# A Gram matrix's mirrored part: identity matmuls on TensorE against 32x32 transposes on VectorE and a round trip through DRAM

## What is computed

```python
# layer 0: softmax attention; q, k have 64 rows, v has 512
q = (Wq @ x + bq).T;  k = Wk @ x2 + bk;  v = Wv @ x2 + bv
attn = softmax(q @ k)          # (1024, 1024), over the keys
x = v @ attn.T + x
# layer 1: attention without softmax
g = (g_w @ x2 + g_b).T; theta = (theta_w @ x + theta_b).T; phi = phi_w @ x2 + phi_b
y = ((theta @ phi) / phi.shape[-1] @ g).T
wy = w_w @ y + w_b
out = bn_gamma * (wy - bn_mean) * rsqrt(bn_var + eps) + bn_beta + x
```

## Time and profile before

| | |
|---|---|
| median of 3 runs | 1039.71 us (1039.63 to 1039.83) |
| profiled execution | 1039.65 us, span 1037.8 us |
| PE busy | 1028.6 us, 99% |
| DVE, ACT, POOL busy | 685.1, 494.9, 296.4 us (66, 48, 29%) |
| moved by DMA | 155.46 MB |

### The profile page before, as it was taken

The page is one execution under the profiler, slowest core; times in us unless marked ns, Lnnn a source line. Parts: engine busy times, 40 slices in busy tenths (PEclk is TensorE's granted clock), DMA queues, the critical chain, the costliest instruction groups (busy, mean ns, idle before and its releaser), DMA issues.

```text
span 1037.8 us, 13692 instructions
## 1 busy us (share of the span) xinstructions
PE 1028.6 (99%) x5055; PEld 850.6 (82%) x5055; DVE 685.1 (66%) x970; ACT 494.9 (48%) x835; POOL 296.4 (29%) x253
## 2 busy tenths in 40 slices
PE   9999999999999999999999999999999999999998
PEld 7778888888888887888888888888887888878887
DVE  6994497834888258882588825887268862688625
ACT  7653564425554264542744427454275532655321
POOL 1652370122701236012360123502144022540220
PEclk9999999999999999999999999999999999999999
DMA  7747153561545514455244552455434464335602
GB/s 255 217 142 234 65 200 123 163 222 54 170 129 189 190 63 161 139 186 183 72 153 152 178 178 87 137 163 181 165 103 136 150 201 142 122 123 163 193 31 81
DMA packets 94226, 155.46 MB, mean 150 GB/s; under 512 B 10064, under 2 KB 43728, under 8 KB 94160
## 3 DMA queue, kind: packets, MB, share of 16 engines
q1 hardware_dynamic: 84944, 137.80, 40.6%
q10 hardware_dynamic: 9216, 16.78, 4.8%
HBM read 104.22 MB, written 50.33 MB: 149 GB/s over the span
## 4 chain that ended last, share of the span: by engine, by line
PE 89%; DVE 4%; POOL 2%; DMA 2%; ACT 1%; issue 1%; SPq 0%; ACTq 0%; DVEq 0%
PE pG L661 33%; PE pG L567 14%; PE pG L672 8%; PE pG L575 6%; PE pG L606 4%; PE pG L582 4%; PE pT L694 3%; PE pG L694 3%; PE pS L618 2%; PE pM L649 2%; PE pT L514 2%; PE pT L618 2%; PE pM L640 2%; PE pS L503 2%; POOL x1s L1067 1%; DMA x2T_f<-in_ctx2T_dram 1%
## 5 line engine op out<-in xcount | busy, mean ns | idle before, releaser
L661 PE MATMUL pG<-pt,vT 128*128 128x512 f32 x1536 | 353.8, 389 | 0.0
L661 PEld LDWEIGHTS pG<-pt,vT 128*128 128x128 f32 x1536 | 286.9, 188 | 58.6
L1103 POOL TENSOR_TENSOR xms<-xr,xms 128x512 fp32r<-128x512 f32 x64 | 87.4, 1372 | 327.6 <-ACT xms L854 327.6
L567 PE MATMUL pG<-wv,x2s 128*128 128x512 f32 x720 | 169.3, 392 | 0.3
L567 PEld LDWEIGHTS pG<-wv,x2s 128*128 128x128 f32 x720 | 133.9, 188 | 31.7 <-issue 2.5
L1019 DVE SCALAR_TENSOR_TENSOR xr<-pG,cl,xr 128x512 f32<-128x512 f32 x64 | 47.9, 749 | 167.8 <-PE pG L661 167.8
L854 ACT ACTIVATE xms<-xr 128x512 fp32r<-128x512 f32 x64 | 40.4, 631 | 174.9 <-DVE xr L1019 174.9
L996 DVE TENSOR_TENSOR pt<-mv,pt 128x512 fp32r<-128x512 f32 x128 | 83.3, 693 | 56.3 <-ACT pt L832 56.1
L1099 POOL TENSOR_TENSOR ys<-yf,ys 128x256 fp32r<-128x256 f32 x32 | 29.6, 926 | 284.0 <-ACT ys L823 284.0
L832 ACT ACTIVATE pt<-mv 128x512 fp32r<-128x512 f32 x128 | 73.3, 622 | 57.9 <-DMA mv<-turn 42.0
L1074 POOL TENSOR_TENSOR x2Ts<-x2T_f,x2Ts 128x512 fp32r<-128x512 f32 x64 | 86.2, 1374 | 37.3 <-ACT x2Ts L792 37.3
(11 more groups left out here) (145 smaller groups left out, 1486.6 us busy)
## 6 DMA issues: line engine op xcount, KB each, us to landing
turn<-tp SPq DMA_DIRECT2D x64, 512.0 KB, 3.2
mv<-turn SPq DMA_DIRECT2D x256, 128.0 KB, 2.9
x2T_f<-in_ctx2T_dram SPq DMA_DIRECT2D x32, 512.0 KB, 4.8
xr<-in_x_dram ACTq DMA_DIRECT2D x64, 256.0 KB, 5.2
st<-in_ctx_dram SPq DMA_DIRECT2D x31, 512.0 KB, 6.4
st<-in_x_dram SPq DMA_DIRECT2D x29, 512.0 KB, 4.2
out_dram<-oh SPq DMA_DIRECT2D x32, 256.0 KB, 2.0
out_dram<-xr SPq DMA_DIRECT2D x31, 256.0 KB, 8.0
```

The lines of the kernel that those rows point to most:

```text
L567: last = mm(bank, x2s[:, l, c, 128 * m:128 * m + 128], wv[:, r, c, :], start=(c == 0 and n == 0), stop=(c == 3 and n == 2))
L661: last = mm(bank, vT[:, l, m, 128 * c:128 * c + 128], pt(h)[:, r, m, :], start=(m == 0 and n == 0), stop=(m == 7 and n == 2))
L1103: done(tt(xms(h)[:, c, LO, :], xr[c][:, :], xms(h)[:, c, HI, :].bitcast(F), ALU.subtract), "xlo")
```

## The change

In images 1 to 7 the eleven identity matmuls go. ACT's do_L writes L into gram_n; DVE transposes each row block of it in 32x32 blocks (do_tl) into tl; SP writes tl to a DRAM scratch `nt` and reads it back with four DMAs into lt; DVE adds lt to gram_f in SBUF (do_gn), after its do_G. The PE transposes GT, ACT's do_G and what follows wait for do_gn (s_gn). The division by the row sums moves from DVE to ACT (do_n; DVE keeps the reciprocal, do_r). The four strings of order are written anew; of the waits of do_tr, that on s_mv becomes one on s_turn. The first image keeps its identity matmuls, with two small swaps in its order.

```diff
-   PE  "... v:0 v:1 psi v:2 S:0 S:1 L:0 L:1 L:2 S:2 S:3 L:3 G:0 G:1 G:2 GT:0 G:3 GT:1 S:4 S:5 v:3 v:4 v:5 v:6 v:7
-        Y:0 S:6 S:7 Y:1 Y:2 Y:3 PV:0,0,0 M:0 ..."
+   PE  "... v:0 v:1 v:2 S:0 S:1 L:0 psi L:1 L:2 S:2 S:3 L:3 G:0 G:1 G:2 G:3 S:4 S:5 v:3 v:4 v:5 GT:0 GT:1 v:6 v:7
+        Y:0 S:6 S:7 Y:1 Y:2 Y:3 PV:0,0,0 M:0 ..."
-   ACT "... acc x2T:5 q v:0 x2T:6 x2T:7 q2 v:1 k2 v:2 S:0 L:0 L:1 S:1 L:2 L:3 S:2 G:0 S:3 G:1 T:0 GT:0 G:2 G:3 GT:1
-        v:3 T:1 v:4 S:4 v:5 v:6 T:2 v:7 S:5 Y:0 T:3 Y:1 Y:2 Y:3 psi S:6 S:7 xr:0 ..."
+   ACT "... x2T:5 q v:0 x2T:6 x2T:7 q2 v:1 k2 acc v:2 S:0 L:0 n:0 L:1 S:1 L:2 n:1 S:2 L:3 n:2 S:3 n:3 T:0 G:0 G:1
+        G:2 G:3 v:3 S:4 n:4 v:4 T:1 S:5 v:5 GT:0 GT:1 n:5 v:6 T:2 v:7 T:3 Y:0 S:6 Y:1 n:6 Y:2 Y:3 psi S:7 n:7 xr:0 ..."
-   DVE "acc k q accl v:0 q2 v:1 k2 S:0 v:2 S:1 n:0 tr:0 n:1 tr:1 S:2 S:3 G:0 n:2 G:1 tr:2 G2:0 G:2 G:3 n:3 G2:1 T:0
-        tr:3 G2:2 G2:3 v:3 GT:0 S:4 v:4 GT:1 T:1 v:5 n:4 S:5 v:6 tr:4 T:2 v:7 Y:0 n:5 tr:5 Y:1 T:3 Y:2 Y:3 S:6 S:7
-        n:6 tr:6 n:7 tr:7 mt ..."
+   DVE "acc k q v:0 q2 v:1 k2 accl S:0 v:2 S:1 r:0 tr:0 tl:0 r:1 tl:1 tr:1 tl:2 S:2 S:3 r:2 tl:3 G:0 tr:2 G:1 r:3 G:2
+        G:3 tr:3 T:0 S:4 gn:0 gn:1 gn:2 gn:3 r:4 v:3 G2:0 G2:1 tr:4 S:5 G2:2 G2:3 v:4 r:5 T:1 v:5 GT:0 GT:1 tr:5 v:6
+        T:2 v:7 T:3 S:6 Y:0 r:6 Y:1 tr:6 S:7 Y:2 Y:3 r:7 tr:7 mt ..."
@@ SP, move(b, p)
+                if b and p == 0:
+                    eng.wait_ge(s_tl, 4 * b)
+                    eng.dma_start(nt, tl[:, :, :]).then_inc(s_nw, 16)
                 for t in range(2):
                     eng.wait_ge(s_turn[2 * p + t], 16 * (b + 1))
                 for k in range(2):
+                    if b and p == 0 and k == 1:
+                        eng.wait_ge(s_nw, 16 * b)
+                        for i in range(4):
+                            eng.dma_start(lt[32 * i:32 * i + 32, :, :], nt[:, i, :].rearrange("(j a) n -> a j n", a=32))\
+                                .then_inc(s_nr, 16)
@@ PE, do_G and do_GT
-                       x2Ts[:, HI, m, G_FROM[r]:512], start=(m == 0), stop=False)
+                              x2Ts[:, HI, m, G_FROM[r]:512], start=(m == 0), stop=(b > 0 and m == 7))
+                if b:
+                    done(last, "g")
+                    return
-                wait_free(eng, b, use_g(b, r))
+                if b:
+                    eng.wait_ge(s_gn, 4 * (b - 1) + r + 1)
@@ ACT: do_v, do_L, do_n, do_G
+                elif m >= 3 and b:
+                    eng.wait_ge(s_nw, 16 * b)
+                done(act(gram_n[:, r, :] if b else gram[:, LO, r, :], bank_of(use_l(b, r)), ACT.Copy), "Lhi")
+            def do_n(b, t):
+                wait(eng, "rec", b, t)
+                done(act(P[:, :], P[:, :], ACT.Copy, scale=rec[:, t:t + 1]), "norm")
             def do_G(b, r):
+                if b:
+                    eng.wait_ge(s_gn, 4 * (b - 1) + r + 1)
@@ DVE: do_tl, do_gn, and do_tr for t >= 4
+            def do_tl(b, r):
+                wait(eng, "Lhi", b, r)
+                n = 256 if r < 2 else 512
+                eng.transpose(tl_row(r), gram_n[:, r, 0:n].rearrange("p (c i m) -> p i c m", i=4, m=32))\
+                    .then_inc(s_tl, 1)
+            def do_gn(b, r):
+                eng.wait_ge(s_nr, 64 * b)
+                if r == 0:
+                    wait_free(eng, b, use_g(b, 3))
+                for i in range(2):
+                    d = max(G_FROM[r] // 128 - 2 * i, 0)
+                    if d < 2:
+                        part = gram_f[r][:, 256 * i:256 * i + 256].rearrange("p (d j m) -> p d j m", d=2, j=4)[:, d:]
+                        last = tt(part, part, lt_pair(i, r)[:, d:], ALU.add)
+                last.then_inc(s_gn, 1)
-                    for i in range(2):
-                        eng.wait_ge(s_mv[t // 2 * 2 - 4 + i], 64 * (b + 1))
+                    eng.wait_ge(s_turn[t - 4], 16 * (b + 1))
```

More of the change, by code:

```diff
@@ L199, in xattn_kernel @@
         mts = at("mts", [128, 2, 2, 256], R, rd + 12288)
+        gram_n = at("gram_n", [128, 4, 512], F, rd + 8192)
+        tl = at("tl", [128, 4, 384], F, ra + 6144)
+        lt = at("lt", [128, 4, 384], F, ra + 22528)
         k1 = at("k1", [128, 1024], F, rd)
@@ L237, in xattn_kernel @@
         s_turn = [sem(f"s_turn{t}") for t in range(8)]
+        nt = nc.dram_tensor("nt", [128, 4, 384], F).ap()
+        s_tl, s_gn = sem("s_tl"), sem("s_gn")
+        s_nw, s_nr = sem("s_nw"), sem("s_nr")
         sems = {n: sem("s_" + n) for n in PER}
@@ L331, in xattn_kernel, with tl_row, lt_pair @@
         gb = lambda k: cl[:, 28 + k:29 + k]
+        def tl_row(r):
+            if r < 2:
+                return tl[:, :, 64 * r:64 * r + 64].rearrange("p i (c m) -> p i c m", m=32)
+            return tl[:, :, 128 * r - 128:128 * r].rearrange("p i (c m) -> p i c m", m=32)
+        def lt_pair(i, c):
+            pair = lt[:, :, 128:384] if i else lt[:, :, 0:128]
+            return pair.rearrange("p j (d n) -> p d j n", d=2)[:, :, :, 32 * c:32 * c + 32]
         def gram_turned(r):
@@ L581, in do_G @@
                 for m in range(8):
-                    mm(bank[:, G_FROM[r]:512], x2Ts[:, HI, m, 128 * r:128 * r + 128],
-                       x2Ts[:, HI, m, G_FROM[r]:512], start=(m == 0), stop=False)
+                    last = mm(bank[:, G_FROM[r]:512], x2Ts[:, HI, m, 128 * r:128 * r + 128],
+                              x2Ts[:, HI, m, G_FROM[r]:512], start=(m == 0), stop=(b > 0 and m == 7))
+                if b:
+                    done(last, "g")
+                    return
                 if b == 0 and r == 0:
@@ L592, in do_GT @@
             def do_GT(b, r):
-                wait_free(eng, b, use_g(b, r))
+                if b:
+                    eng.wait_ge(s_gn, 4 * (b - 1) + r + 1)
+                else:
+                    wait_free(eng, b, use_g(b, r))
                 for c in range(r + 1, 4):
@@ L806, in do_L @@
                 wait(eng, "g", b, use_l(b, r))
-                done(act(gram[:, LO, r, :], bank_of(use_l(b, r)), ACT.Copy), "Lhi")
+                done(act(gram_n[:, r, :] if b else gram[:, LO, r, :], bank_of(use_l(b, r)), ACT.Copy), "Lhi")
+            def do_n(b, t):
+                wait(eng, "rec", b, t)
+                done(act(P[:, :], P[:, :], ACT.Copy, scale=rec[:, t:t + 1]), "norm")
             def do_G(b, r):
-                wait_free(eng, b, use_g(b, r))
+                if b:
+                    eng.wait_ge(s_gn, 4 * (b - 1) + r + 1)
+                else:
+                    wait_free(eng, b, use_g(b, r))
                 if b and r >= 2:
@@ L861, in do_th @@
                 done(act(th[:, HI, k, 512 * h:512 * h + 512], bank_of(i), ACT.Identity, bias=thb(k)), "thhi")
-            do = dict(w=do_w, xr=do_xr, x2=do_x2, x2a=do_x2a, xs=do_xs, x1=do_x1, k=do_k, q=do_q, k2=do_k2, q2=do_q2, v=do_v, S=do_S, L=do_L, G=do_G,
+            do = dict(w=do_w, xr=do_xr, x2=do_x2, x2a=do_x2a, xs=do_xs, x1=do_x1, k=do_k, q=do_q, k2=do_k2, q2=do_q2, v=do_v, S=do_S, n=do_n, L=do_L, G=do_G,
                       GT=do_GT, Y=do_Y, x2T=do_x2T, acc=do_acc, psi=do_psi, T=do_T, mts=do_mts, B=do_B, xc=do_xc, PV=do_PV,
@@ L950, in do_S, with do_r, do_n @@
                 done(eng.tensor_reduce(nmax[:, t:t + 1], s_bank(t)[:, :, :], AX.XY, ALU.max, negate=True), "mx")
-            def do_n(b, t):
+            def do_r(b, t):
                 wait(eng, "exp", b, t)
                 done(eng.reciprocal(rec[:, t:t + 1], rsum[:, t:t + 1]), "rec")
+            def do_n(b, t):
+                do_r(b, t)
                 wait(eng, "rec", b, t)
@@ L970, in do_G @@
                 done(tt(gram_f[r][:, G_FROM[r]:512], bank_of(i)[:, G_FROM[r]:512],
-                        gram[:, LO, r, G_FROM[r]:512].bitcast(F), ALU.add), "gf")
+                        gram_n[:, r, G_FROM[r]:512] if b else gram[:, LO, r, G_FROM[r]:512].bitcast(F), ALU.add), "gf")
+            def do_tl(b, r):
[13 more added lines that the diff above has]
+                last.then_inc(s_gn, 1)
             def do_G2(b, r):
                 wait(eng, "Ghi", b, r)
-                if r >= 2:
+                if r >= 2 and b == 0:
                     wait(eng, "g", b, use_g(b, 3))
@@ L1053, in _ @@
             do = dict(w=do_w, consts=do_consts, acc=do_acc, accl=do_accl, x2=do_x2, x1=do_x1, x2T=do_x2T, k=do_k, q=do_q, k2=do_k2, q2=do_q2, v=do_v,
-                      S=do_S, n=do_n, tr=do_tr, G=do_G, G2=do_G2, GT=do_GT, Y=do_Y, T=do_T, mt=do_mt, mts=do_mts, B=do_B, PV=do_PV, th=do_th,
+                      S=do_S, n=do_n, r=do_r, tr=do_tr, tl=do_tl, gn=do_gn, G=do_G, G2=do_G2, GT=do_GT, Y=do_Y, T=do_T, mt=do_mt, mts=do_mts, B=do_B, PV=do_PV, th=do_th,
                       wy=do_wy, out=do_out)
```

## The result

The changed kernel took 1128.37 us (median; 1124.65 to 1129.84), the kernel before 1039.67 beside it: ratio 1.0849, 95% interval 1.0821 to 1.0877. It is slower by 88.7 us. The prediction had the direction and 65 us of it: 1104.5, in a range from 1080 to 1125.

What follows compares the result with a forecast made beforehand. PE, busy 99% of the span, was taken as the bound. Per image 10.1 us of stalls plus 0.2 switching less 1.03 saved gave 9.3, 65 over seven images: 1104.5 us, range 1080 to 1125.

Steps and rivals of the forecast that it cites:

- The eleven matmuls: On PE at G: removing eleven identity matmuls saves 1.03 us an image, 7.2 us in seven images.
- The stalls: On PE, images 1 to 7: new waits for other engines' results total 10.1 us an image.
- the five places: PE waits: G:1 for ACT's L:3, G:3 for DVE's G:1, v:5 for DVE's v:3, Y:3 for Y:1, PV for Y:2.
- To v:5: PE before v:5 waits 3.0 us for DVE's v:3, behind gn and r:4, which waits for ACT's exp:4.
- T:0: On DVE before S:4 and gn: T:0 follows tr:3 at 9.8 and ends 11.3 us after G:0 starts.
- SP's queue: DMA issues on SP: nt and lt stand ahead of reads for T:1 to T:3, costing nothing by itself.
- the round trip: DMA write of nt and reads into lt: 8.3 us, between 7.5 and 10.5, landing at 12.4 after G:0.
- To v:6: PE before v:6 waits 1.3 us for DVE's v:4, behind G2, tr:4 and the maximum of S:5.
- the sum, made at full clock: Per image: 10.1 of stalls plus 0.2 switching less 1.03 gives 9.3 us; seven images 65 us.
- The rival: Slower clock: PE falls to 1.2 GHz behind stalls before v:5 and PV, 19 us more, 1123; chance 0.11.
- Switching: An added 0.2 us an image on PE, beside the stalls, in the sum.
- New operations: Durations: DVE transposes 0.65 and 0.35, additions 2.05, ACT division 1.1, nt write 3.9, lt reads 4.4 us.

Runs made afterwards that it cites:

- the last pair of runs: Kernel before with the fastest reordered kernel's orders and division on ACT, keeping its eleven matmuls, no nt or lt: 1038.08 us; beside that reordered changed kernel: 1033.6 us.
- The run with fillers: Changed kernel plus unread matmuls where PE waits, twelve before v:5 and eight before PV:0,0,0: 1114.0 us, ratio 1.0723.
- the best one: Changed kernel with new orders for images 1 to 7, S tiles in pairs, Y:0 ahead of S:6 S:7, lt at its own address: 1033.6 us, ratio 0.9948.

## Why the prediction was right and where it failed

- *The eleven matmuls, 1.03 an image:* right in size (1.16 at G by the last pair of runs, of which 0.73 reached the period), and a gain only where nothing waits.
- *The stalls, 10.1 an image:* measured 65.1 / 7 = 9.3, in the five places and for the reasons given. G:1 1.28 (1.6 predicted), G:3 0.31 (0.5), Y:3 0.45 (0.9), PV 2.55 (2.75) all came out a little shorter than their sums, by links that overlap (the maxima of S:2 and S:3, 1.2 each, start 1.11 apart). v:5 with v:6 came out longer, 4.7 against 4.3.
- *To v:5, stall 3.0:* mis-sized, in two terms that came out level. The first is T:0. It was taken as starting right behind tr:3 and ending at 11.3; its reads of turn landed late behind the write of nt, and it ended at 12.9. The prediction checked SP's queue for T:1 to T:3 and not for T:0, whose reads come next behind the very issue. The second is the round trip, put at 8.3 and at 10.5 at most: it took 9.8 to 9.9 in three images, 10.2 in one and 10.8 to 11.6 in the three in which gn waits for it. gn began at 13.9 instead of 12.5. The run without the trip puts both together at 2.05 in the third image.
- *To v:6, stall 1.3:* it didn't show, since v:5 ran at half clock through it; at full clock it was there with 1.0.
- **The failed step is the sum, made at full clock.** Waits of 3.0 and 2.75 us in front of a PE that had not waited once in images 1 to 7 were priced at their length, and the work behind them at its old speed. The runs showed it at 1.2 GHz behind thirteen of fourteen such waits, 23.7 us, of which 15 to 17 are the net price. The rival had it, with mechanism and places, and was given 0.11 because the trace of before has no wait of this length. That trace did show nine matmuls at half rate behind an idle PE, which was evidence for the rival; against it stood one wait of 1.66 in the first image, behind which the clock stayed up (line at the end), little beside waits of 3. Its size, 19, came near by two errors: v:5 was given 0.7 an image and cost 1.2 net (2.15 less the 1.0 of v:6), PV was given 2 and cost 1.2.
- *Switching, 0.2 an image:* the second term too small. The edges beside the five waits cost some 7 us in all, 1.0 an image. The run with fillers shows what a sum at full clock should have given: about 1114, not 1104.5.
- The rival's 1123 with v:5's term mended, (4.7 - 4.3) x 7 = 3, is 1126, and 1128.4 was measured. This is partly luck, for its waits are too long (73.7 with the mended term, 65.1 measured) and its edges too short (1.4 for 7).
- *New operations:* the division took 1.15 (1.1 predicted), tl 0.40 and 0.67 (0.35, 0.65), gn 1.97 (2.05), nt landed after 4.0 (3.9). lt's reads landed after 4.0 each in the median, but from the first issue to the last landing they took 5.8 to 7.6, where 4.4 was taken and 5.7 was the upper bound. DVE's transposes cost what the row of before gave for their size, 0.67 for four blocks. The figure of the Trainium skill (VectorE: DVE Perf Modes, The three transpose paths), 311 ns for a block in bf16, would make 1.24 of them, an estimate that this trace doesn't bear out.

## What to carry to other kernels

Where one engine is busy all the time, a change that frees it 1 us must first be laid out against the moments at which it asks for the other engines' results; here the same change is 8.5% slower or 0.5% faster by the order of the queues (and the address of one tile). Price a wait that is put in front of PE in two ways, with the work behind it at full and at the lower clock: in this kernel the lower one came behind most waits of 2.1 to 5.9 us. When a DMA is put into a queue, look first at what is issued right behind it, and count a round trip to its last landing.

## What was not expected of the hardware

- The clock fell behind most waits of 2.1 us (six of seven in the run without the trip) and of 2.55 us (six of seven in the changed kernel, five of seven both in the run without the trip and in the one with v:3 ahead of gn), but not behind each: the same wait of 2.55 left it up at 493.05 in the changed kernel. In the run with fillers, where PE had worked up to the last wait, one of 2.48 left it up and another took it down, and one of 1.88 took it down. Behind waits of 0.9 to 1.7 in the later images no group was slow. In the first image Y waits for 1.65 to 1.81 in the traces of all fourteen kernels, and there the clock stayed up in six, among them the kernel before and the best one, and fell in eight, among them the changed kernel (lines below). What tells the cases apart wasn't found.
- The reads of turn issued 0.45 us behind the 768 KB write of nt landed 3.9 to 4.3 after their issue and held ACT's T:0 for 2.0 us (at 321.56). In the median of all a read lands after 3.0, and the same four took 2.5 to 3.0 in the run without the write.
- S tiles (64-row matmuls) cost 0.89 each alone and 1.59 in a pair, from start to next start.

The same 36 matmuls of the first image in the kernel before, at full clock, and in the changed kernel, partly at half:

```profile
60.95 4.91 PE L606 MATMUL pG<-wpg,gram 128*128 128x256 f32 x36 [1.66 <-DVE vT L946]
61.10 6.03 PE L637 MATMUL pG<-wpg,gram 128*128 128x256 f32 x36 [1.81 <-issue]
```
